# An adaLN and 4-bit FFN kernel: first stage reordered on four queues, sums of the last two pairs interleaved, last M6 in a bank of its own

## What is computed

```python
q_emb = relu(cond @ W3 + b3)                              # (64, 512)
z     = (64 * x + x.sum(axis=1, keepdims=True)) * q_emb[:, None, :]
x1    = relu(z @ W2 + b2)                                 # (64, 64, 512)
w_up   = ((codes_up - 7.5) * repeat(scale_up, 64)).T      # 4-bit codes as int32, 512 x 2048
y1    = x1 @ w_up + b_up + x1 @ lora_a @ lora_b
x2    = relu(y1)
out   = x + x2 @ w_down + b_down + x2 @ lora_a2 @ lora_b2 # w_down likewise, 2048 x 512
```

## Time and profile before

| what | value |
|---|---|
| median of 3 executions | 765.12 us (764.54 to 765.32) |
| the profiled execution, its own time | 765.55 us |
| its span, first to last instruction | 763.7 us |
| PE busy | 740.0 us, 97% of the span |
| PEld busy | 609.5 us, 80% |
| DVE busy | 554.5 us, 73% |
| ACT busy | 420.4 us, 55% |
| POOL busy | 78.3 us, 10% |
| mean granted TensorE clock | 0.993 |

### The profile page before, as it was taken

How to read it: one execution, slowest core, us unless ns; L and a number is a source line. 1 busy time by engine, 2 the same in 40 slices (tenths; PEclk the granted TensorE clock), 3 DMA queues, 4 the chain that set the end, 5 groups by cost and what they waited for, 6 DMA issues and landing times. The chain is left out here.

```text
span 763.7 us, 9568 instructions
## 1 busy us (share of the span) xinstructions
PE 740.0 (97%) x3248; PEld 609.5 (80%) x3248; DVE 554.5 (73%) x725; ACT 420.4 (55%) x727; POOL 78.3 (10%) x68
## 2 busy tenths in 40 slices
PE   6599999999999999999999999999999999999997
PEld 5478888878878878888888888888888888888876
DVE  6598866776976487767776877767776877757585
ACT  3866175574754175666647265666656363626531
POOL 0063524333430000000000000000000000000000
PEclk9899999999999999999999999999999999999999
DMA  8957978988628696655516798766515696665552
GB/s 325 308 185 218 292 214 264 288 262 250 221 99 290 210 383 230 220 194 193 180 56 229 254 385 265 222 202 192 180 56 183 229 382 220 199 192 194 193 165 111
DMA packets 92160, 170.60 MB, mean 223 GB/s; under 512 B 8528, under 2 KB 25040, under 8 KB 91472
## 3 DMA queue, kind: packets, MB, share of 16 engines
q1 hardware_dynamic: 91824, 169.90, 67.4%
q10 hardware_dynamic: 288, 0.08, 0.0%
HBM read 130.10 MB, written 40.89 MB: 224 GB/s over the span
## 5 line engine op out<-in xcount | busy, mean ns | idle before, releaser
L1138 PE MATMUL ps<-x_hi,ring 128*128 128x512 f32 x672 | 262.1, 390 | 3.0 <-DVE x_lo L932 1.8
L1139 PE MATMUL ps<-x_lo,ring 128*128 128x512 f32 x672 | 261.5, 389 | 0.0
L1140 PE MATMUL ps<-x_hi,ring 128*128 128x512 f32 x672 | 261.4, 389 | 0.0
L1138 PEld LDWEIGHTS ps<-x_hi,ring 128*128 128x128 f32 x672 | 126.1, 188 | 31.4 <-DVE x_lo L932 2.7
L1140 PEld LDWEIGHTS ps<-x_hi,ring 128*128 128x128 f32 x672 | 126.1, 188 | 26.3
L1139 PEld LDWEIGHTS ps<-x_lo,ring 128*128 128x128 f32 x672 | 126.1, 188 | 26.1
L388 ACT ACTIVATE xt<-xt,gated,gate_n 128x64 f32<-128x64 f32 x216 | 74.6, 430 | 37.2 <-DVE gated L741 37.2
L497 ACT ACTIVATE f<-ps,bias 128x512 f32<-128x512 f32 x96 | 64.8, 690 | 42.2 <-PE ps L1140 42.2
L932 DVE TENSOR_TENSOR x_lo<-x_sum,x_hi 128x512 fp32r<-128x512 f32 x96 | 76.8, 818 | 4.2 <-ACT x_hi L535 3.4
L853 DVE TENSOR_TENSOR ps<-s,ps 128x512 f32<-128x512 f32 x48 | 33.3, 693 | 51.1 <-PE ps L1140 50.7
L890 DVE TENSOR_TENSOR res<-ps,res 128x512 f32<-128x512 f32 x72 | 48.3, 687 | 23.6 <-PE ps L1140 23.2
(11 more groups left out here) (80 smaller groups left out, 1002.0 us busy)
## 6 DMA issues: line engine op xcount, KB each, us to landing
ring<-made_w SPq DMA_DIRECT2D x336, 256.0 KB, 3.7
made_w<-made SPq DMA_DIRECT2D x16, 1280.0 KB, 6.0
xt<-in_x SPq DMA_DIRECT2D x32, 256.0 KB, 5.6
code<-in_codes SPq DMA_DIRECT2D x16, 512.0 KB, 8.3
scale<-made_s SPq DMA_DIRECT2D x16, 512.0 KB, 8.0
res<-in_x SPq DMA_DIRECT2D x4, 2048.0 KB, 10.1
made_w<-plain SPq DMA_DIRECT2D x64, 128.0 KB, 6.3
out<-res SPq DMA_DIRECT2D x12, 512.0 KB, 5.5
```

Source lines behind the costliest of these rows:

```text
L1138: pe.matmul(dest, w_hi, a_hi, start=start, stop=False, skip_group_check=True)
L1139: pe.matmul(dest, w_hi, a_lo, start=False, stop=False, skip_group_check=True)
L1140: return pe.matmul(dest, w_lo, a_hi, start=False, stop=stop, skip_group_check=True)
```

## The change

On SP, `w3` is loaded in two parts, the tables are 96 rows instead of 128, the first two units read their scales directly from the input (two rows outermost, each repeated 64 times), the DRAM copy of the scales is issued near the end, and SP waits for it before the third unit's scales. Tiles 3, 4, 7 are modulated through ScalarE instead of 4, 6, 7. The order of the steps changes on ScalarE and VectorE, and `low_rank(0)` runs after `j` = 0. In the last slots the steps of pairs 6 and 7 alternate. At the very end M6 starts its own bank, ScalarE copies what M1 left in BP to the SBUF tile `s4`, and VectorE adds `s4` to the result tile.

```diff
-    ON_DVE, ON_ACT = (0, 1, 2, 3, 5), (4, 6, 7)
+    ON_DVE, ON_ACT, SUMMED = (0, 1, 2, 5, 6), (3, 4, 7), (0, 1, 3, 2, 4, 5, 7, 6)
...
+        THREE = 3 * QUAD
...
             def load_scale(u):
                 if u >= 3:
                     sp.wait_ge(dequantized, u - 3 + 1)
-                rows = made_s[uid(FIRST[u])].rearrange("h c v -> (h c) v").unsqueeze(1)
-                sp.dma_start(scale[u % 3][:], rows.to_broadcast([2 * COPIES, P // 2 // COPIES, 1024])).then_inc(scale_loaded[u % 3], 16)
+                if u < 2:
+                    rows, each = scales[uid(FIRST[u])], 2
+                else:
+                    rows, each = made_s[uid(FIRST[u])].rearrange("h c v -> (h c) v"), 2 * COPIES
+                sp.dma_start(scale[u % 3][:], rows.unsqueeze(1).to_broadcast([each, P // each, 1024])).then_inc(scale_loaded[u % 3], 16)
...
-            sp.dma_start(raw_w3[:], w3[:]).then_inc(cond_loaded, 16)
-            for k in range(KD):
-                load_x(0, k)
-                sp.dma_start(raw_w2[:, k, :], w2[:, k, :]).then_inc(w2_raw[k], 16)
-                if k == 1:
-                    sp.dma_start(made_s, scales.unsqueeze(2).to_broadcast([UNITS, 2, COPIES, 1024])).then_inc(scales_copied, 16)
-            sp.dma_start(raw_tables[:], tables[:]).then_inc(tables_loaded, 16)
-            load_x(0, KD)
-            load_x(0, KD + 1)
+            sp.dma_start(raw_w3[:, :, 0:P], w3[:, :, 0:P]).then_inc(cond_loaded, 16)
+            load_x(0, 0)
+            load_raw_w2(0)
+            sp.dma_start(raw_w3[:, :, P:D], w3[:, :, P:D]).then_inc(w3_loaded, 16)
+            load_x(0, 1)
+            load_raw_w2(1)
+            load_x(0, 3)
+            load_x(0, 2)
+            load_raw_w2(2)
+            load_raw_w2(3)
+            load_x(0, 4)
+            sp.dma_start(raw_tables[0:THREE], tables[:]).then_inc(tables_loaded, 16)
+            load_x(0, 5)
             load_codes(0)
+            load_scale(0)
+            load_x(0, 7)
+            load_x(0, 6)
+            load_codes(1)
+            load_scale(1)
+            sp.dma_start(made_s, scales.unsqueeze(2).to_broadcast([UNITS, 2, COPIES, 1024])).then_inc(scales_copied, 16)
+            load_codes(2)
             sp.wait_ge(scales_copied, 16)
-            load_scale(0)
-            load_x(0, KD + 2)
-            load_x(0, KD + 3)
-            for u in (1, 2):
-                load_codes(u)
-                load_scale(u)
+            load_scale(2)
             sp.wait_ge(w2_split, KD)
...
-                for t, (a, j) in enumerate(((1, 0), (0, 1), (0, 0), (1, 1))):
+                for t, (a, j) in enumerate(((1, 0), (0, 1)) + (((1, 1), (0, 0)) if dd else ((0, 0), (1, 1)))):
...
             x_high(0, 1)
             w2_high(2)
+            x_modulate(0, 3)
             x_high(0, 2)
             w2_high(3)
             x_high(0, 3)
...
             x_modulate(0, 4)
             x_high(0, 4)
-            x_modulate(0, 6)
             z_tile(0, 0, 0, 0)
...
             x_high(0, 7)
+            plain_high(0)
             act.copy(wide_flat[:, T:], raw_wide[:, T:]).then_inc(tab_cast, 1)
-            plain_high(0)
...
                     if n == 13 and last:
-                        x2_high(s, 6, 3)
+                        x2_high(s, 6, 2)
+                        x2_high(s, 7, 2)
+                    if n == 14 and last:
                         x2_high(s, 6, 4)
-                    if n == 14 and last:
-                        x2_high(s, 7, 3)
                         x2_high(s, 7, 4)
...
-            pass_c11(*before)
+
+            act.wait_ge(prod[M1], chain_no(SBS - 1, LAST[-1]) + 1)
+            act.copy(s4[:], ps[4 * (before[1] % 2) + BP][:]).then_inc(q_down_done, 1)
...
-            x_sum(0, 0)
-            x_shift(0)
-            x_modulate(0)
-            w2_low(0)
-            x_sum(0, 1)
-            x_shift(1)
-            x_low(0, 0)
...
+            for k in range(2):
+                x_sum(0, k)
+                x_shift(k)
+                x_modulate(k)
+                w2_low(k)
+                x_low(0, k)
+            x_sum(0, 3)
+            x_gate(0, 3)
             x_sum(0, 2)
             x_shift(2)
-            x_low(0, 1)
             x_modulate(2)
             w2_low(2)
-            x_sum(0, 3)
-            x_shift(3)
             x_low(0, 2)
-            x_modulate(3)
-            w2_low(3)
             x_sum(0, 4)
             x_gate(0, 4)
+            w2_low(3)
             x_low(0, 3)
             lora_low()
             wide_low(slice(0, T), 2)
             x_sum(0, 5)
             x_shift(5)
             x_modulate(5)
-            x_sum(0, 6)
-            x_gate(0, 6)
+            x_low(0, 4)
             x_sum(0, 7)
             x_gate(0, 7)
+            x_low(0, 5)
             dequantize(0)
-            x_low(0, 4)
+            x_sum(0, 6)
+            x_shift(6)
+            x_modulate(6)
             add_lora(0)
-            x_low(0, 5)
+            x_low(0, 6)
             x1p_low(0, 0)
             x1p_low(0, 2)
-            x_low(0, 6)
-            dequantize(1)
             x_low(0, 7)
             plain_low(0)
+            dequantize(1)
...
+            add_lora(1)
             wide_low(slice(T, NH * P), 3)
-            add_lora(1)
             x1p_low(1, 0)
             x1p_low(1, 2)
...
                     if n == 12 and last:
                         x2_total(s, 6, 0)
-                        x2_total(s, 6, 1)
+                        x2_total(s, 7, 0)
                     if n == 13 and last:
-                        x2_total(s, 7, 0)
-                        x2_total(s, 7, 1)
-                        x2_low(s, 6, 3)
+                        x2_low(s, 7, 1)
+                        x2_low(s, 6, 2)
                     if n == 14 and last:
-                        x2_total(s, 7, 3)
-                        x2_low(s, 7, 2)
-                        x2_low(s, 7, 3)
+                        x2_low(s, 6, 4)
+                        x2_low(s, 7, 4)
...
             finish_c22(SBS - 1, 1)
+            to = res[:, 3, 1, :]
+            dve.wait_ge(q_down_done, down_no(SBS - 1, 3, 1) - 8 + 1)
+            dve.wait_ge(res_summed, 4 * (SBS - 2) + 4)
+            dve.tensor_tensor(to, to, s4[:], ALU.add).then_inc(res_summed, 1)
+            dve.wait_ge(res_summed, 4 * (SBS - 2) + 5)
+            add_res(*before, BQ)
             add_res(*before, BP)
-            add_res(*before, BQ)
...
             for m in range(KD):
+                if m == 1:
+                    pe.wait_ge(w3_loaded, 16)
...
-                    if j == 1 and k in (0, KD - 1):
-                        low_rank(k // 3)
+                low_rank(j)
...
-            tail(*before)
+
+            n = len(LAST) - 1
+            wait_bank(pe, BQ, SBS - 1, n)
+            product(SBS - 1, n, M6, BQ, True)
+            pe.wait_ge(q_down_done, down_no(SBS - 1, 3, 1) - 8 + 1)
+            product(SBS - 1, n, M7, BP, False)
```

More of the change, by code:

```diff
@@ L46, in adaln_ffn, with sum_no @@
             ("U", 5), ("U", 6), ("U", 7), ("D", 2, 0), ("D", 2, 1), ("D", 3, 0), ("D", 3, 1)]
-    ON_DVE, ON_ACT = (0, 1, 2, 3, 5), (4, 6, 7)
+    ON_DVE, ON_ACT, SUMMED = (0, 1, 2, 5, 6), (3, 4, 7), (0, 1, 3, 2, 4, 5, 7, 6)
+    def sum_no(s, t):
+        return SUMMED.index(t) + 1 if s == 0 else 8 * s + t + 1
     def gate_no(s, t):
@@ L144, in adaln_ffn @@
         raw_tables = sb("raw_tables", [P, 2 * D + NH * P], F32, "res")
-        wide_flat, raw_wide = wide[:].rearrange("p h c -> p (h c)"), raw_tables[:, 2 * D:2 * D + NH * P]
+        THREE = 3 * QUAD
+        lora_flat, raw_lora = lora[0:THREE].rearrange("p v d -> p (v d)"), raw_tables[0:THREE, 0:2 * D]
+        wide_flat, raw_wide = wide[0:THREE].rearrange("p h c -> p (h c)"), raw_tables[0:THREE, 2 * D:2 * D + NH * P]
         raw_w2 = sb("raw_w2", [P, KD, D], F32, "x2")
@@ L163, in adaln_ffn @@
         code_loaded = [sem(f"code_loaded{v}") for v in range(3)]
-        scales_copied = sem("scales_copied")
+        scales_copied, w3_loaded = sem("scales_copied"), sem("w3_loaded")
         scale_loaded = [sem(f"scale_loaded{v}") for v in range(3)]
@@ L280, in load_scale, with load_raw_w2 @@
                     sp.wait_ge(dequantized, u - 3 + 1)
-                rows = made_s[uid(FIRST[u])].rearrange("h c v -> (h c) v").unsqueeze(1)
-                sp.dma_start(scale[u % 3][:], rows.to_broadcast([2 * COPIES, P // 2 // COPIES, 1024])).then_inc(scale_loaded[u % 3], 16)
+                if u < 2:
[3 more added lines that the diff above has]
+                sp.dma_start(scale[u % 3][:], rows.unsqueeze(1).to_broadcast([each, P // each, 1024])).then_inc(scale_loaded[u % 3], 16)
+            def load_raw_w2(k):
+                sp.dma_start(raw_w2[:, k, :], w2[:, k, :]).then_inc(w2_raw[k], 16)
             def store_plain(u):
@@ L559, in _ @@
             act.wait_ge(tables_loaded, 16)
-            act.copy(lora[:].rearrange("p v d -> p (v d)"), raw_tables[:, 0:2 * D]).then_inc(tab_cast, 1)
+            act.copy(lora_flat, raw_lora).then_inc(tab_cast, 1)
```

(47 more changed lines are left out.)

2 lines of the change are left out of this document (removed).

## The result

The changed kernel takes 768.66 us (median of 20 executions) against 765.68 for the kernel before (20 executions beside it). One of the 20 executions of the changed kernel, a slow one, took 1924.8 us and is left out of the ratio, which goes by the mean of the others: 1.0029, 95% interval 1.0017 to 1.0042. It is slower, by 0.29%, where 758.7 was forecast; the range ended at 763.0. The profiled execution took 768.97 us with a span of 766.9, against 765.55 and 763.7.

A forecast was written before the change was run, and what follows sets the result against it. The prediction took TensorE's holes at both ends, mainly from VectorE's order, as the bound, the middle being full. Front -3.1 and tail -3.3 made -6.4 us: 759.15 for the profiled execution, 758.7 as median, range 754.0 to 763.0.

The forecast's parts named there:

- The tail: End of the kernel: TensorE's three waits and their clock cost go away, -3.3 us, between 0 and -3.4.
- The front up to tile 5: Start of the kernel: TensorE starts at about 11, and the W2 product's second half at 26.0 instead of 30.84.
- The term "+0.1": Start of the W2 product with w3 split: taken as 11, between 10.4 and 11.4, against 10.90 before.
- The loads: SP's queue: first codes at 19.0, two-row scale load on two engines 10.3 us, tile 7 landing at 30.1.
- 1.44 MB fewer ahead, 4.5 us: Ahead of tiles 6 and 7, scales copy and a quarter of the tables go: first codes at 19.0, not 23.4.
- The front from tile 7 on: From tile 7's sum at 30.1 to the first weight unit at 45.4 instead of 49.66; front -3.1 us with clock.
- The 1.2 us for clock and the unit's third tile: First weight unit: allowance for low clock and a late third tile, 1.2 us, between 0.4 and 2.5.
- What SP does behind its wait: SP waits for the scales copy till about 45; later weight stores cost nothing, or 1 to 2 us without cover.
- The second: Scale loads: two engines at 16.5 GB/s each, late loads hold the first unit's third tile; 769.1 us, chance 0.07.
- The first: Scale loads: the two-row load is as fast as any, tile 7 lands at 22.6; 755.2 us, chance 0.20.
- The third: Last slots: the tail's waits come back elsewhere, VectorE having about 10 us in slot 13; 762.0 us, chance 0.08.
- the last thing to watch: Last sign of being wrong: waits between 50 and 80 us behind SP's late stores.

The follow-up runs named there:

- the run of the tail alone: Kernel before with only the last slots' edits (steps of pairs 6 and 7 alternating, M6 in its bank): 762.41 us against 765.78, ratio 0.9959.
- the scales spread: Changed kernel with each of the first two scale loads issued as two DMAs of one row repeated 64 times: 757.07 us, ratio 0.9899.
- the run with full tables: Changed kernel with the tables' load of 128 rows again instead of 96: 765.17 us, ratio 0.9994.

## Why the prediction was wrong, point by point

**The tail: right.** -3.3 was forecast; -3.4 stands in the profile and in the run of the tail alone.

**The front up to tile 5: the working right, the split of w3 mis-sized.** The 15 us of VectorE from the first matmul to the second half were measured at 28.19 - 13.13 = 15.06. But the start was put between 10.4 and 11.4 and came at 13.13: the first 6 us moved 113 GB/s, against 179 in the run with w3 whole. The term "+0.1" was 2.2.

**The loads: the two-row load right, the bytes ahead of it not.** The split over two engines was taken and held: tile 7's sum comes 33.01 - 21.4 = 11.6 us after the first codes, 11.1 were forecast. "1.44 MB fewer ahead, 4.5 us" failed: the codes came 2.0 us sooner, not 4.5. I counted the cut of the tables by bytes; it made that load slower, and with 128 partitions the codes land at 19.6, near the 19.0 of the forecast. This row of after shows the sum of tile 7 behind its load:

```profile
33.01 0.69 DVE L750 TENSOR_REDUCE sums<-xt 128x8 f32<-128x512 f32 x1 [4.88 <-DMA xt<-in_x]
```

**The front from tile 7 on: right.** 15.3 us from that sum to the first weight unit were forecast, 14.9 measured; the late sum, 33.01 instead of 30.1, alone makes it 47.93 instead of 45.4. The 1.2 us for clock and the unit's third tile came as 1.28.

**What SP does behind its wait: the step that failed.** It had the right chain (wait for the copy, stores of W2, weight stores, ScalarE's buffer) and the price "nothing", 1 to 2 us without cover. It cost 6.67. The stores were to end 4 us after ScalarE wants their buffer, and the unit that needs the result was to start about 69. They ended 9.16 us after, and TensorE stood from 72.16 on. The buffer was wanted hardly earlier than before (62.16 against 62.51); the stores were late, by 7.8 us at their issue (57.0 against 49.21) and by 3.7 in landing (11.6 against 7.9). Of the 7.8 us, 2.2 are VectorE's: SP holds the residual's load, which goes ahead of these stores, for the wide table's low part, and that ends at 51.02 instead of 48.80. The others come from the copy: it was thought to end about 45 and ended at 48.7, behind codes that came 2.4 us late and the second two-row load, and everything written behind SP's wait in the program goes out late with it, also what needs no scales. What the sum left out is the queue: all of that goes out at once and the stores land behind it. Issued 4.5 us earlier, with W2's stores first, they landed 0.8 us earlier; with the scales spread they were issued at 47.38 and took 8.1 us. How much SP's wait and the queue each weigh stays open; that the two-row loads are behind both is shown. The wait of 4.21 us also has a clock price, some 2.5 us here, which was counted for the front and not for this place.

**The sum.** Against the forecast of -6.4 the profiled execution has +3.4. Of the 9.8 between, 6.67 are the wait near 72 us with its clock, 2.65 the later front (-0.45 at the first LoRA product instead of -3.1), the tail gives 0.1 back, and 0.6 are spread over the middle and the time outside the span.

**The rivals.** The second, slower by a rate of 16.5 GB/s, did not happen: each engine moved about 27 GB/s, near the 25.5 taken. The first would have been the change's result with another form of load: 757.07 measured, 755.2 forecast for it. The third (the tail's waits elsewhere) did not happen. "Slower" came by a case that was named as the last thing to watch and had no chance of its own; that slower had 0.07 was for rival 2, another mechanism.

## What to carry to other kernels

When a load is slow, price what its queue issues behind it as well as who waits for its data: here the two-row load by itself cost 5.1 us in the kernel before, and what the queue behind such loads brought late cost 6.7 in the kernel after. A cover read in the trace of before holds for the queue of before: work out anew when the buffer is wanted and when its store lands. A wait of TensorE can cost clock on top: 4.21 us cost some 2.5 more here, 3.35 us in the run with full tables none. Count a load by the rate of its own form, not by its bytes: fewer partitions took longer here, and so did two parts in place of one load.

## What was not expected of the hardware

- SP stood 7.33 us at the issue of two x tiles and 11.94 at that of the copy, each right behind a two-row load in its queue; with the scales spread, they were issued in 1.06 and 0.61 us. For the first, the two-row load was queued and not yet the one that slowed the queue (9.51 to 16.84 us against 24 to 32). What SP stood for is not shown.
- A load of 96 partitions with rows of 12 KB moved 218 GB/s at a DMA share of 1.00, and one of 128 partitions with the same rows 410. The Trainium skill ("DMA: Bandwidth & Descriptors", "Why a DMA increments its semaphore by 16 and not by 1") counts 16 engines for 96 partitions, as for 128, so that rule does not account for it. The slow rate goes with the 96 rows in the kernels that load them, and no run here shows why.
- w3 in two parts held the first 6 us to 113 GB/s, against 179 in one. Whether it is the size of the pieces or the queue's order at the start wasn't tried apart.
